# One transformer block on one core: V's projection in one piece, transposes and a key product moved, a shorter last block

## The reference

```python
def attention(xq, xkv, wq, wk, wv, wo, bo):          # scale 64 ** -0.5
    ...
    attn = softmax(einsum('bihd,bjhd->bhij', q, k) * scale)
    return einsum('bhij,bjhd->bihd', attn, v) @ wo + bo
h = layernorm(x, ln1);  x = attention(h, h, sa...) + x
h = layernorm(x, ln2);  x = attention(h, cond, ca...) + x
h = layernorm(x, ln3);  p = h @ ff_w1 + ff_b1;  a, gate = halves of p
x = a * gelu(gate) @ ff_w2 + ff_b2 + x
```

## Time and profile before

| | us |
|---|---|
| median of 3 runs | 993.49 (992.88 to 995.5) |
| the profiled execution: its own time | 995.91 |
| its span, first to last instruction | 994.1 |
| mean granted TensorE clock | 0.998 of full |

### The profile page before, as it was taken

The page is one execution under the profiler, slowest core; times in us unless marked ns, Lnnn a source line. Parts: engine busy times, 40 slices in busy tenths (PEclk is TensorE's granted clock), DMA queues, the critical chain, the costliest instruction groups (busy, mean ns, idle before and its releaser), DMA issues.

```text
span 994.1 us, 29745 instructions
## 1 busy us (share of the span) xinstructions
PE 959.2 (96%) x12770; PEld 752.8 (76%) x12770; DVE 809.8 (81%) x928; ACT 632.4 (64%) x1171; POOL 435.2 (44%) x408
## 2 busy tenths in 40 slices
PE   8999999999999999999999999988999999999997
PEld 6677777777777777777777777755788889888886
DVE  4689998999988899999999999998859898454433
ACT  4767766777787777767777666886745454333322
POOL 5116554465544356755456644451432355600000
PEclk9999999999999999999999999999999999999999
DMA  7696466476354746635563574593110011100000
GB/s 180 175 193 159 108 113 135 91 144 153 64 136 84 166 92 144 137 77 138 108 143 94 106 145 92 122 221 59 50 44 1 1 30 36 43 1 22 22 22 22
DMA packets 178115, 96.28 MB, mean 97 GB/s; under 512 B 141120, under 2 KB 158016, under 8 KB 177600
## 3 DMA queue, kind: packets, MB, share of 16 engines
q1 hardware_dynamic: 177984, 94.38, 42.7%
HBM read 56.60 MB, written 12.58 MB: 70 GB/s over the span
## 4 chain that ended last, share of the span: by engine, by line
PE 79%; DVE 10%; ACT 5%; issue 4%; POOL 1%; DVEq 0%; ACTq 0%; POOLq 0%
PE W L683 25%; PE SC L654 14%; PE SC L763 9%; PE W L619 8%; PE W L710 5%; PE W L773 4%; PE W L629 4%; PE W L943 3%; DVE nmax L1280 3%; PE SC L751 3%; DVE PR L1285 2%; DVE OTF L1291 1%; ACT OTF L1045 1%; PE W L696 1%; ACT PR L1029 1%
## 5 line engine op out<-in xcount | busy, mean ns | idle before, releaser
L1029 ACT ACTIVATE PR<-SC,nmax 128x1024 f32<-128x1024 f32 x256 | 285.6, 1116 | 152.3 <-DVE nmax L1280 150.1
L1280 DVE TENSOR_REDUCE nmax<-SC 128x1 f32<-128x1024 f32 x256 | 304.4, 1205 | 35.2 <-PE SC L654 33.6
L1285 DVE STREAM_TRANSPOSE PR<-PR 128x1024 f32<-128x1024 f32 x256 | 313.0, 1231 | 9.0 <-ACT PR L1029 2.1
L683 PE MATMUL W<-PR,V 32*64 32x256 f32 x8192 | 240.1, 378 | 4.4 <-issue 1.0
L654 PE MATMUL SC<-QKT 64*128 64x512 f32 x768 | 226.8, 418 | 4.0 <-ACT PR L1029 3.6
L683 PEld LDWEIGHTS W<-PR,V 32*64 32x64 f32 x8192 | 195.1, 132 | 45.7 <-issue 30.4
L654 PE MATMUL SC<-QKS 64*128 64x512 f32 x768 | 225.9, 418 | 3.4 <-ACT PR L1029 2.8
L507 POOL TENSOR_TENSOR X<-f_raw,X 128x512 f32<-128x512 f32 x128 | 161.3, 1290 | 145.5 <-ACT f_raw L1057 145.5
L654 PEld LDWEIGHTS SC<-QKT 64*128 64x128 f32 x768 | 131.1, 185 | 34.0 <-ACT PR L1029 12.3
L654 PEld LDWEIGHTS SC<-QKS 64*128 64x128 f32 x768 | 130.9, 185 | 32.9 <-ACT PR L1029 12.8
L495 POOL TENSOR_TENSOR OTF<-OTF 128x512 f32<-128x512 f32 x28 | 36.1, 1288 | 183.8 <-ACT OTF L1045 183.8
(11 more groups left out here) (140 smaller groups left out, 1624.6 us busy)
## 6 DMA issues: line engine op xcount, KB each, us to landing
V<-scratch_v SPq DMA_DIRECT2D x128, 256.0 KB, 4.8
QKS<-QKT SPq DMA_DIRECT2D x96, 256.0 KB, 4.1
scratch_v<-VST SPq DMA_DIRECT2D x32, 256.0 KB, 3.5
wo<-in_L_xattn_sa_wo_dram SPq DMA_DIRECT2D x64, 64.0 KB, 3.5
f_raw<-in_L_xattn_ff_w_dram SPq DMA_DIRECT2D x12, 256.0 KB, 2.9
X<-in_x_dram SPq DMA_DIRECT2D x4, 512.0 KB, 4.9
w_raw<-in_L_xattn_sa_wk_dram SPq DMA_DIRECT2D x16, 128.0 KB, 4.8
w_raw<-in_L_xattn_sa_wq_dram SPq DMA_DIRECT2D x16, 128.0 KB, 3.8
```

The source lines that it names most:

```text
L683: last = mm(W[cols, a, on:on + 2 * P], V4[s][rows, blk, :], PR[rows, NT * s:NT * s + NT, Q * blk:Q * blk + Q], start=(blk < 2), stop=(blk ...
L1029: nc.scalar.activation(PR[:, NT * s + t, :], SC[t % 2][:, :], ACT.Exp, bias=nmax[:, t % 4:t % 4 + 1], accum_out=den[:, s, t:t + 1]).then_i ...
L1280: V.tensor_reduce(nmax[:, t % 4:t % 4 + 1], SC[t % 2][:, :], AX, ALU.max, negate=True).then_inc(d_max, 1)
L1285: V.transpose(tile, tile).then_inc(d_tr, 1)
```

## The change

1. **Prologue.** SP issues the key weights ahead of `load_w(0)`. TensorE does `raw_kv(0)` by halves: the first in front of `turn_rows`, the second in place of the second `keep_busy`, in front of the projections. ScalarE copies the halves out in front of `gain_x` and behind the first q/k copy. `place(0, 1)` moves ahead of the 1 MB store of the keys and waits for the first scores.
2. **V.** In heads 2 to 28 all of V's quarter stands in tile 0, behind the q/k projection there.
3. **Transposes.** For heads 1 to 30 the transpose of tile 6 moves from tile 7 to behind the next head's rowmax 0, that of tile 0 from tile 1 to behind rowmax 2.
4. **Moved work.** `project_out(h-2, 3)` moves ahead of the turning of wq; ScalarE copies wq's first two turned blocks out in tile 1 of head 30 instead of tile 0.
5. **Last block.** The last gate and gated product stand behind the parts of block 30. The last `ff_down` signals at its half; the adds and stores go by two row tiles each.

```diff
@@ sync
+            for dst, src in zip((wk_a, wk_b), cw(ca_wk)):
+                sp.dma_start(dst, src).then_inc(m_kv[0], 16)
             load_w(0)
             load_wv(0)
-            for m, w in enumerate((ca_wk, ca_wv)):
-                for dst, src in zip(((wk_a, wk_b), (wv_a, wv_b))[m], cw(w)):
-                    sp.dma_start(dst, src).then_inc(m_kv[m], 16)
+            for dst, src in zip((wv_a, wv_b), cw(ca_wv)):
+                sp.dma_start(dst, src).then_inc(m_kv[1], 16)
...
             place(0, 0)
+            sp.wait_ge(s_sc, 2)
+            place(0, 1)
             sp.wait_ge(a_pre, 4)
             sp.dma_start(KV_d[0], flat(12, 2)).then_inc(m_kvs, 16)
-            place(0, 1)
...
-            for q in range(2 * B):
+            for q in range(2 * B - 1):
...
+            for i in range(2):
+                sp.wait_ge(d_fx, 4 * B - 1 + i)
+                tiles = slice(NT - 4 + 2 * i, NT - 2 + 2 * i)
+                sp.dma_start(by_row(out, B - 1)[:, tiles, :], X[:, B - 1, tiles, :]).then_inc(m_out, 16)
@@ tensor: ff_down, prologue, heads
-                last.then_inc(s_w2, 1)
+                    if i == 3 or i == 1 and F == 2 * B * NF - 1:
+                        last.then_inc(s_w2, 1)
...
+            pe.wait_ge(a_cnd, 1)
+            raw_kv(0, (0,))
             for r in range(2):
                 pe.wait_ge(d_z, 4 * r + 4)
...
-                keep_busy(SC[1], 6)
+                if r == 0:
+                    keep_busy(TP[0], 6)
+            raw_kv(0, (1,))
             for n in range(NQ):
                 project(0, n, WB[n])
-            pe.wait_ge(a_cnd, 1)
-            raw_kv(0)
...
-                    if (h, t) in V_AT:
+                    if h < 2 and (h, t) in V_AT:
...
-                        project_v(u, i, W[:, bank, :], (1,) if h > 1 and t == 1 else (0, 1))
+                        project_v(u, i, W[:, bank, :])
...
                     if t == 0 and h > 1 and (h, 1) in V_AT:
...
-                        project_v(u, i, W[:, bank, :], (0,))
+                        project_v(u, i, W[:, bank, :])
...
+                    if t == 0 and h - 2 in PLAIN:
+                        pe.wait_ge(a_op, 4 * (h - 2) + 2)
+                        project_out(h - 2, 3)
                     if (h, t) in TURN_W:
...
-                    if t == 0 and h - 2 in PLAIN:
-                        pe.wait_ge(a_op, 4 * (h - 2) + 2)
-                        project_out(h - 2, 3)
@@ scalar
             act.wait_ge(m_gb[0], 32)
+            raw_kv(0, (0,))
...
                 split_qkv(0, n, WB[n])
-            raw_kv(0)
+                if n == 0:
+                    raw_kv(0, (1,))
...
-                        if t == 0 and at in TURN_W:
+                        if t == HS - 1 - h and at in TURN_W:
...
-                if 2 <= F < 2 * B * NF:
+                if 2 <= F < 2 * B * NF - 1:
                     gate(F)
...
                 nc.scalar.copy(PT[0][:, (F - 1) % NPT, :], U32[(F - 1) % 2]).then_inc(a_uh, 1)
+                if F == 2 * B * NF - 1:
+                    gate(F)
@@ vector
                     if h > 0 and t == 0:
+                        if h > 1:
+                            turn(h - 1, NT - 2)
                         turn(h - 1, NT - 1)
+                    if h > 0 and t == 2:
+                        turn(h, 0)
...
-                    if t > 0 and not (t == 3 and h > 0 or t in (5, 6) and summing):
+                    if t > 0 and not (t in (1, 3) and h > 0 or t in (5, 6) and summing or t == 7 and 0 < h < HS - 1):
                         turn(*divmod(NT * h + t - 1, NT))
...
-                    dve.wait_ge(s_w2, NF * (q + 1))
                     for i in range(2):
+                        dve.wait_ge(s_w2, NF * (q + 1) + (i if q == 3 else 0))
```

More of the change, by code:

```diff
@@ L439, in _ @@
                       .then_inc(m_f[n % 2], 16)
-            for q in range(2 * B):
+            for q in range(2 * B - 1):
                 sp.wait_ge(d_fx, 2 * (q + 1))
                 sp.dma_start(by_row(out, q // 2)[:, by_tile(q), :], X[:, q // 2, by_tile(q), :]).then_inc(m_out, 16)
-            sp.wait_ge(m_out, 32 * B)
+            for i in range(2):
+                sp.wait_ge(d_fx, 4 * B - 1 + i)
+                tiles = slice(NT - 4 + 2 * i, NT - 2 + 2 * i)
+                sp.dma_start(by_row(out, B - 1)[:, tiles, :], X[:, B - 1, tiles, :]).then_inc(m_out, 16)
+            sp.wait_ge(m_out, 32 * B + 16)
         @block.gpsimd
@@ L584, in keep_busy, with raw_kv @@
                     nc.tensor.transpose(bank[:, 0:P], ident[:, :], ident[:, :])
-            def raw_kv(m):
+            def raw_kv(m, halves=(0, 1)):
                 pe.wait_ge(m_kv[m], 32)
@@ L590, in raw_kv @@
                     pe.wait_ge(a_pre, 2)
-                for half in range(2):
+                for half in halves:
                     cols = slice(half * BANK, (half + 1) * BANK)
@@ L621, in project, with project_v @@
                 last.then_inc(s_qkv, 1)
-            def project_v(u, i, bank, parts=(0, 1)):
-                if i == 0 and 0 in parts:
+            def project_v(u, i, bank):
+                if i == 0:
                     pe.wait_ge(p_wv, u + 1)
-                for j in parts:
+                for j in range(2):
                     for c, (l, r) in enumerate(TERMS):
@@ L630, in project_v @@
                                       wv_s[r][:, k, :], start=(c == 0 and k == 0), stop=(c == 2 and k == KD - 1))
-                if 1 in parts:
-                    last.then_inc(s_v, 1)
+                last.then_inc(s_v, 1)
             def scores(h, t):
@@ L811, in _ @@
                         turn_kv(1, (TP[1], MISC))
-                    if (h, t) in V_AT:
+                    if h < 2 and (h, t) in V_AT:
                         u, i, bank = V_AT[h, t]
[L814 to L817, removed]
-                        project_v(u, i, W[:, bank, :], (1,) if h > 1 and t == 1 else (0, 1))
+                        pe.wait_ge(d_qkv, t + 1 if h == 0 else NQ + 2)
+                        project_v(u, i, W[:, bank, :])
                     for g, n, bank in [] if t == 7 and early(h) else PROJ_AT.get((h, t), []):
@@ L1481, in _ @@
                                 PT[0][:, (F - 1) % NPT, :].bitcast(F32), sub).then_inc(d_ul, 1)
+                if F == 2 * B * NF - 1:
+                    gated(F)
                 if F in LN_FF:
```

## The result

| | before | after |
|---|---|---|
| median, us | 993.18 | 979.16 (977.26 to 979.76, 4 runs) |
| ratio, 95% interval | | 0.985 (0.9831 to 0.987) |
| span of the profiled execution, us | 994.1 | 977.2 |

14.0 us shorter by the medians; 15.55 were forecast. The spans differ by 16.8, because the profiled execution of before was one of its long ones. It has three stalls of TensorE: 0.67 us in head 7 and 0.65 in head 28 (read from the distance of the two bursts, 5.91 and 5.88 for 5.24), and this one in head 30. The trace after has none of them.

What follows compares the result with a forecast made beforehand. TensorE was taken to bound a head, ScalarE a few tenths behind. 3.3 + 8.75 - 0.9 + 1.0 + 1.4 + 2.0 = 15.55 us off 993.49 gave 977.9 us; range 974.0 to 985.5.

Steps and rivals of the forecast that it cites:

- What bounds a head: In each head: TensorE binds, ScalarE a few tenths behind, VectorE with 1.15 us to spare.
- the wait of 0.33: ScalarE's wait for VectorE's rowmax before exp(h, 0), 0.33 us, expected to go with the shifted transposes.
- 0.35 a head: Heads with V in one piece: 0.35 us won in each, between 0.2 and 0.48.
- The rival of TensorE alone: In the heads, ScalarE keeps up: 25 x 0.48 = 12 us rather than 8.75, giving 974.6; chance 0.07.
- The term: Heads 2 to 28 without 13 and 14: 25 heads at 0.35 us each, 8.75 us won.
- The shift costs nothing: Moved transposes: rowmax 1 waits for later scores 1, but VectorE arrives with them; cost nothing, up to 0.71 a head.
- The slower rival: VectorE at rowmax 1: later scores 1 push what follows, 27 x 0.71 = 19.2 us lost, 1005.0; chance 0.04.
- Heads 13 and 14: There project_out(h-2, 3) comes later behind all of V and ScalarE waits: 0.45 us lost in each, 0.9 together.
- Head 30 and the clock: Head 30: moving wq's copies behind exp(30, 0) wins 1.0 us; the clock staying at full wins 1.4 more.
- The prologue: the step that failed: Start of the kernel: key product moved forward, its weights landing at 9.4, wins 3.3 us (1.9 to 3.9).
- Last block: End of the kernel: earlier gated product, split adds and stores win 2.0 us (1.6 to 2.6).

Runs made afterwards that it cites:

- V alone: Kernel before with V in one piece and the transposes where they were: 995.75 us, ratio 1.0024.
- the long filler: 30 or 32 instead of 12 identity transposes in front of the key product or first turning; with 32 in the changed kernel 978.28 us, ratio 0.9845.
- `project_out` first: Changed kernel with project_out(h-2, 3) ahead of the q/k projection and V in tile 0 of heads 13, 14 and 31: 976.18 us, ratio 0.9826.
- the halves behind the turns: Changed kernel with the halves of the key product behind the first and second turning of rows: 977.93 us, ratio 0.9841.

## Why the prediction was right, and where not

- *What bounds a head.* The text named TensorE, with ScalarE a few tenths behind. In fact two chains met within 0.03 us, and V alone gains nothing. The sum did not suffer, because it asked for the wait of 0.33 to go by the shift: rowmax 0 starts earlier, as said, and this gives the most. (Of the distances between first bursts 20 lie between 20.74 and 20.97, not 19.)
- *0.35 a head.* Measured 0.43, and the path was the one named: V's copy on ScalarE is what the burst waits for last. Mis-sized was what ScalarE wins. The text took the length of its wait, 0.33; but an exponential that does not wait starts 0.12 before the f_raw copy ends (197.82 against 197.94), so exp(h, 0) comes 0.44 sooner (18.01 behind the burst before it, where it was 18.45). The rival of TensorE alone came close in its number, by another path. The term came to 12.6 rather than 8.75: 7.8 from the 18 heads like 8, 0.3 each from heads 10, 11 and 27, 0.4 from head 29, 1.3 from head 2, nothing from head 12, and 1.0 and 1.2 from heads 7 and 28. In these two 1.3 are the stalls of before, which is chance; without them the term is 11.3.
- *The shift costs nothing.* Right: rowmax 1 follows its transposes without a gap and VectorE keeps 0.53 of its wait, where 0.7 was said. The slower rival named the right place, rowmax 1, but VectorE's spare time did not run out there.
- *Heads 13 and 14.* The mechanism was right, ScalarE's wait grew from 0.92 to 1.38; 0.34 each rather than 0.45.
- *Head 30 and the clock.* The two heads became 3.4 us shorter, but 1.0 of it is the stall of before. The other 2.4 are as forecast: 1.0 of wait, 0.5 for the scores behind it at the lower clock, and 0.94 in head 31, where the slow burst counts. The clock stayed at full in head 30 in all eight traces with the wait of 0.86, and fell in five of the six with 1.83. By the rule of the Trainium skill (TensorE: Matmul & The Clock Gate, Part 4: PE-mode transpose) it would have fallen as before, since the turns of wq stayed; it did not.
- *The prologue: the step that failed.* "I take 9.4; then the first half ends at 11.4" was the landing of the weights; it was 10.37, near the late bound of 10.8, which by the text's own sum leaves some 2.3 of the 3.3. And the sum had no term for the clock, though the heads had shown what a wait can do: at 1.2 GHz, eight turns and six fillers took 3.1 us where they take 1.6. Nothing was left in this trace. Where the clock held in both places the prologue won 1.1 to 2.4 us, not 3.3, against old prologues that differ by 0.6 among themselves. In the best of them the landing was 9.58, but the scores of head 0 were ready at 28.93 rather than 28.05, because the projections started 0.4 later and the copies of q and k landed 0.4 later than the sum has it.
- *Last block.* 1.4 for 2.0: the chain from the last `ff_up` to the last add shrank by 1.33 rather than 1.6, since the last `ff_down` took 1.7 us and not 1.5; half the bytes saved 0.1 at the store, not 0.4.

```profile
971.15 0.69 DVE L1498 TENSOR_TENSOR PT_lo<-GU,PT_hi 128x512 fp32r<-128x512 f32 x1 [0.69 <-ACT PT_hi L1240]
972.98 1.33 DVE L1523 TENSOR_TENSOR X<-W,X 128x512 f32<-128x512 f32 x2 [1.14 <-PE W L780]
```

The errors had opposite signs, +3.3 in the prologue against -3.9 in the heads, 1.3 of it stalls. That the median landed 1.3 us from the forecast is in part luck.

## What to carry to other kernels

When a chain of waits runs over one engine, look at the start of each link for another engine that ends in the same tenth of a microsecond; shorten that one too, or little is won. An operation that another engine waits for goes ahead of filler work on its own engine: moving two transposes behind a row maximum was worth 8.6 us, without an instruction less. A step moved into a wait is worth its length only if its data is there and the clock holds; put in the sum what the clock costs, with a chance. With more fillers in the wait the clock held in all four traces, though no median shows a gain.

## What the runs showed that I had not expected

The clock's fall behind a wait is not settled by the kernel: the same code lost it in one execution and kept it in another. The 14 traces, by what TensorE waits for (us of idle time just before):

| wait | us | traces | clock fell to 1.2 GHz in |
|---|---|---|---|
| first turning, old prologue | 2.35 to 2.52 | 5 | 0 |
| key product or turning, new prologue or its variant, 12 fillers | 1.90 to 2.44 | 5 | 2 (2.41 and 2.44) |
| the same with 30 or 32 fillers | 0 to 0.54 | 4 | 0 |
| copies of q and k, key product moved forward | 1.02 | 9 | 2 |
| exponential of head 30, wq copied before it | 1.82 to 1.83 | 6 | 5 |
| the same, wq copied behind it | 0.86 | 8 | 0 |

So the length of the wait alone does not decide: 2.52 kept the clock and 1.02 lost it. What does decide is open. With the long filler 14 of 16 runs had a mean clock of 0.999 or more; of the changed kernel, `project_out` first and the halves behind the turns with 12 fillers, 5 of 12. The means do not tell in which place it was lost.
